# Splitting the attention output product into three fp32r passes, with the second layer's weights loaded late, in a two-layer kernel on one Trainium2 core

## What is computed

```python
def reference(...):
    # layer 0: attention, then a mixture of experts
    q = rmsnorm(x @ Wq); k = rmsnorm(x @ Wk); v = x @ Wv           # 16 heads of 64
    bias = -max(i - j, 0) * softplus(omega) * slope * softplus(k.u)  # per head and key
    attn = softmax(q k^T / 8 + bias, causal)
    y = (attn v).reshape(B, T, H * D) @ Wproj                      # 1024 -> 256
    ...
    # layer 1: a memory read (W_K, W1, W2) and a feed-forward with routed blocks
    ...
```

## Time and profile before

| what | value |
|---|---|
| time, median of 3 runs | 1443.78 us (1443.22 to 1446.7) |
| the profiled execution | 1444.28 us, its span 1442.5 us |
| PE busy | 1380.5 us, 96% of the span, 9680 instructions |
| DVE busy | 991.6 us, 69% |
| ACT busy | 915.8 us, 63% |
| mean granted TensorE clock | 0.98 of full |
| data moved | 122.90 MB, mean 85 GB/s |

### The profile page before, as it was taken

The page is one execution under the profiler, slowest core; times in us unless marked ns, Lnnn a source line. Parts: engine busy times, 40 slices in busy tenths (PEclk is TensorE's granted clock), DMA queues, the critical chain, the costliest instruction groups (busy, mean ns, idle before and its releaser), DMA issues.

```text
span 1442.5 us, 28165 instructions
## 1 busy us (share of the span) xinstructions
PE 1380.5 (96%) x9680; PEld 1087.5 (75%) x9680; DVE 991.6 (69%) x3164; ACT 915.8 (63%) x2292; POOL 168.4 (12%) x562
## 2 busy tenths in 40 slices
PE   4779999999999999999999999999999799999998
PEld 3567778777777777787777777777777578888997
DVE  6938885888588768858875788588578665555442
ACT  5738784878488757848784877578577624433332
POOL 4501110110101101100110111011101100000000
PEclk8879999999999999999999999999999899999999
DMA  6542332232222313222231233132222212111100
GB/s 230 197 146 81 102 97 82 83 113 85 83 81 96 102 63 102 97 76 88 93 104 57 92 113 101 63 100 69 67 94 72 57 57 58 41 41 41 41 16 30
DMA packets 88303, 122.90 MB, mean 85 GB/s; under 512 B 8561, under 2 KB 74466, under 8 KB 88162
## 3 DMA queue, kind: packets, MB, share of 16 engines
q1 hardware_dynamic: 87842, 121.11, 26.1%
q10 hardware_dynamic: 320, 0.00, 0.0%
HBM read 101.69 MB, written 19.40 MB: 84 GB/s over the span
## 4 chain that ended last, share of the span: by engine, by line
PE 87%; ACT 4%; DVE 1%; issue 1%; DMA 0%; SPq 0%; ACTq 0%; DVEq 0%
PE at L799 19%; PE at L808 11%; PE at L884 10%; PE at L859 8%; PE at L925 8%; PE at L1471 7%; PE at L1507 6%; PE at L813 3%; PE at L911 2%; PE at L894 2%; PE at L851 2%; PE at L839 2%; PE at L844 2%; ACT L1065 1%; ACT probT L1056 1%; PE at L1490 1%
## 5 line engine op out<-in xcount | busy, mean ns | idle before, releaser
L1047 ACT ACTIVATE prob<-prob,low 128x512 f32<-128x512 f32 (+3 forms) x512 | 280.6, 550 | 70.9 <-DVE low L1180 70.8
L1180 DVE CUSTOM_DVE_ANT_0 prob<-at,mask 128x512 f32<-128x512 f32 (+3 forms) x512 | 220.5, 487 | 78.9 <-PE at L813 78.9
L1056 ACT ACTIVATE probT<-at 128x512 f32<-128x512 f32 (+1 forms) x256 | 131.6, 541 | 123.2 <-PE at L859 123.1
L808 PE MATMUL at<-kT,qT 64*128 64x512 f32 (+3 forms) x1024 | 194.2, 461 | 8.8 <-DVE up_lo L1233 5.0
L799 PE MATMUL at<-w_hi,cT_lo 128*128 128x386 f32 x512 | 197.5, 386 | 5.1 <-DVE area_raw L1129 4.3
L799 PE MATMUL at<-w_lo,cT_hi 128*128 128x386 f32 x512 | 175.0, 342 | 0.0
L799 PE MATMUL at<-w_hi,cT_hi 128*128 128x386 f32 x512 | 175.0, 342 | 0.0
L859 PEld LDWEIGHTS at<-ident,prob 128*128 128x128 f32 x1280 | 142.4, 141 | 40.0 <-issue 36.7
L859 PE MATMUL at<-ident,prob 128*128 128x128 f32 x1280 | 164.4, 275 | 2.1 <-DVE prob L1193 1.9
L1193 DVE TENSOR_SCALAR prob<-prob,rec 128x512 f32<-128x512 f32 (+3 forms) x512 | 163.3, 383 | 4.5
L884 PE MATMUL at<-probT,v 128*64 128x512 f32 (+3 forms) x1024 | 152.2, 439 | 0.1
(11 more groups left out here) (219 smaller groups left out, 2571.5 us busy)
## 6 DMA issues: line engine op xcount, KB each, us to landing
area_w<-in_L_ffn_w SPq DMA_DIRECT2D x64, 1024.0 KB, 5.5
bias<-in_L_ffn_w SPq DMA_DIRECT2D x160, 32.0 KB, 3.7
x_in<-in_L_attn_x SPq DMA_DIRECT2D x8, 512.0 KB, 6.4
xr<-in_L_attn_x SPq DMA_DIRECT2D x8, 512.0 KB, 4.1
eo_d<-eo SPq DMA_DIRECT2D x32, 128.0 KB, 1.8
x_d<-xr SPq DMA_DIRECT2D x8, 512.0 KB, 2.9
area_raw<-x_d SPq DMA_DIRECT2D x8, 512.0 KB, 4.1
out<-area_raw SPq DMA_DIRECT2D x8, 512.0 KB, 3.0
```

The costliest lines, as they stand in the source:

```text
L808: eng.matmul(bS[i][:, at:at + (c + 1) * P], qT[rows, c * P:(c + 1) * P], kT[rows, 0:(c + 1) * P], start=True, stop=False)
L1047: eng.activation(sl, sl, ACT.Exp, scale=-1.0, bias=low[:, i:i + 1], accum_out=den[:, i:i + 1]).then_inc(exp_done.sem, 1)
L1056: eng.activation(probT[h][:, x:y], bR[i][:, 0:y - x], ACT.Copy).then_inc(done.sem, 1)
L1180: eng.tensor_tensor_reduce(out=prob[s % 2][h][:, off[c]:off[c + 1]], in0=bS[i][:, at:at + (c + 1) * P], in1=mask[:, (NT - 1 - c) * P:T], s ...
```

## The change

The change does these things.

- `output` runs three fp32r matmuls where one fp32 matmul stood: (`yT_lo`, `wp_hi`), (`yT_hi`, `wp_lo`), (`yT_hi`, `wp_hi`), 24 for one n and 96 for a batch.
- `Wproj` goes to `proj_in` in stage 1 and is split there in two halves: two ACT copies of 128x1024 (in the last two rounds, b = 6 and 7) and two POOL subtractions.
- ACT's `copy_y` now writes `yT_hi`, and a new `copy_y` on DVE subtracts it from the bank to get `yT_lo`. `y_done` is now signalled by DVE. The DVE step stands between `divide(s, 0)` or `add_bias` and `copy_q`.
- To make room, the second layer's weights have no tiles of their own. `w1n` is loaded in turn 55 into the token tiles of even batches, `w2n` in turn 62 into `area_w1`, and `rn`, `m1n`, `m2n`, `wk` at the end of turn 63 into `area_w2`, when the last expert is done. `qkn` shares its place with `sq`, for which ACT's `square` gets a wait on `turn_k` of the pair before.
- The jobs have another order: first the four of `w1n`, the four of `w2n`, then the small ones; one job in each slot of turns 62 and 63, and four in turn 64. `scores_210` waits for the job of slot 0 in place of slot 1's. Job 8 waits for the four small loads, and the last job also for the one before it.

```diff
-        w_proj=sb("w_proj", [P, HP, C]),
+        wp_hi=sb("wp_hi", [P, HP, C], F32R),
+        wp_lo=sb("wp_lo", [P, HP, C], F32R),
...
+                    if b >= 6:
+                        half_h = slice((b - 6) * (H // 4), (b - 5) * (H // 4))
+                        eng.wait_ge(wp_load.sem, wp_load.at(0))
+                        eng.activation(wp_hi[:, half_h, :], proj_in[:, half_h, :], ACT.Copy).then_inc(wp_hi_done.sem, 1)
...
+                        eng.tensor_tensor(wp_lo[:, half_h, :], proj_in[:, half_h, :], wp_hi[:, half_h, :].bitcast(F32), ALU.subtract)
...
-        qkn = sb("qkn", [P, NT, 4 * D])
+        qkn = sq
...
-        jobs_at = {(NTURN - 2, 0): (0, 1), (NTURN - 2, 1): (2, 3), (NTURN - 2, 2): (4,), (NTURN - 2, 3): (5,),
-                   (NTURN - 1, 0): (6,), (NTURN - 1, 1): (7,), (NTURN - 1, 2): (8,), (NTURN - 1, 3): (9,),
-                   (NTURN, 0): (10,), (NTURN, 1): (11,)}
+        jobs_at = {(NTURN - 2 + n // 4, n % 4): (n,) for n in range(8)}
+        jobs_at.update({(NTURN, 0): (8, 9), (NTURN, 1): (10, 11)})
...
+                    if s == NTURN - 1:
+                        eng.wait_ge(pe_eo.sem, pe_eo.at(E - 1))
+                        for dst, src in ((rn, t["L1_ffn_router_w"]), (m1n, t["L1_attn_W1"]),
+                                         (m2n[:, :, :], t["L1_attn_W2"].rearrange("(k p) m -> p k m", p=P)),
+                                         (wk[:, :, :], t["L1_attn_W_K"].rearrange("(k p) c -> p k c", p=P))):
+                            eng.dma_start(dst, src).then_inc(small_load.sem, 16)
...
-                    for n in jobs_at.get((s, 1), ()):
+                    for n in jobs_at.get((s, 0), ()):
                         eng.wait_ge(prep_done.sem, prep_done.at(n))
...
-                        m = eng.matmul(bQ[n % 2][:, 0:C], yT[:, h, n * P:(n + 1) * P], w_proj[:, h, :],
-                                       start=(h == 0), stop=(h == HP - 1))
+                        for y, w in ((yT_lo, wp_hi), (yT_hi, wp_lo), (yT_hi, wp_hi)):
+                            m = eng.matmul(bQ[n % 2][:, 0:C], y[:, h, n * P:(n + 1) * P], w[:, h, :],
+                                           start=(h == 0 and y is yT_lo), stop=(h == HP - 1 and y is yT_hi and w is wp_hi))
...
+                        if n == 8:
+                            eng.wait_ge(small_load.sem, small_load.at(0))
+                        if srcs is None:
+                            eng.wait_ge(prep_done.sem, prep_done.at(n - 1))
...
-                    eng.activation(yT[:, s % HP, :], bY[:, :], ACT.Copy).then_inc(y_done.sem, 1)
+                    eng.activation(yT_hi[:, s % HP, :], bY[:, :], ACT.Copy).then_inc(y_hi_done.sem, 1)
...
+                def copy_y(s):
+                    eng.wait_ge(pe_o.sem, pe_o.at(s // HP - 1))
+                    eng.wait_ge(y_hi_done.sem, y_hi_done.at(s))
+                    eng.tensor_tensor(yT_lo[:, s % HP, :], bY[:, :], yT_hi[:, s % HP, :].bitcast(F32), ALU.subtract).then_inc(y_done.sem, 1)
...
                     if begins_in(s) is not None:
                         add_bias(begins_in(s))
+                    if s > 0:
+                        copy_y(s - 1)
                     prepare(s, 2)
```

More of the change, by code:

```diff
@@ L145, in attention_constants @@
         q_scale=sb("q_scale", [P, 1]),
[L146 to L147 removed]
+        **tokens, **early,
         qaug=sb("qaug", [P, T], F32R),
@@ L159, in second_layer_inputs @@
     return dict(
-        w1n=sb("w1n", [P, HC, C]),
-        w2n=sb("w2n", [P, KC, HC * P]),
-        wk=sb("wk", [P, KC, C]),
-        m1n=sb("m1n", [M1, C]),
-        m2n=sb("m2n", [P, KC, M1]),
-        rn=sb("rn", [NB, C]),
         rb=sb("rb", [P, NB]),
@@ L205, in route_tokens @@
         raw_w = sb("raw_w", [P, KC, 3, H * D])
+        proj_in = sb("proj_in", list(wp_hi.shape))
         u_in = sb("u_in", [P, H, D])
@@ L585, in attend @@
     HC, M1, NB = g["HC"], g["M1"], g["NB"]
-    w1n, w2n, wk, m1n, m2n, rn, backT = (g[k] for k in ("w1n", "w2n", "wk", "m1n", "m2n", "rn", "backT"))
+    backT = g["backT"]
     ident = g["ident"]
     xnT_hi_d, xnT_lo_d, x1_d = g["xnT_hi_d"], g["xnT_lo_d"], g["x1_d"]
-    w_hi, w_lo, w_proj, mask, pos, omega, q_scale, W = (g[k] for k in (
-        "w_hi", "w_lo", "w_proj", "mask", "pos", "omega", "q_scale", "W"))
+    w_hi, w_lo, wp_hi, wp_lo, mask, pos, omega, q_scale, W = (g[k] for k in (
+        "w_hi", "w_lo", "wp_hi", "wp_lo", "mask", "pos", "omega", "q_scale", "W"))
     xT_hi, xT_lo, qaug, kaug, ag, tok, bias2 = (g[k] for k in ("c_hi", "c_lo", "qaug", "kaug", "ag", "tok", "bias2"))
@@ L622, in attend @@
         rec = sb("rec", [P, 2 * NT])
-        area_y = sb("area_y", [P, HP * T])
-        yT = area_y[:, :].rearrange("p (h n) -> p h n", h=HP)
+        outs, hidden32 = share(nc, ctx, "area_y", (("yT_hi", [P, HP, T], F32R), ("yT_lo", [P, HP, T], F32R)),
+                               (("hT", [P, HC, T], F32),))
+        yT_hi, yT_lo = outs["yT_hi"], outs["yT_lo"]
         xr = sb("xr", [P, NT, C])
@@ L682, in attend @@
         sp, m1T, rT, number = (l2[k] for k in ("sp", "m1T", "rT", "number"))
-        jobs = [((m1T[:, :, :],), M1, [m1n[:, k * P:(k + 1) * P] for k in range(KC)]),
-                ((rT[:, :, :],), NB, [rn[:, k * P:(k + 1) * P] for k in range(KC)]),
-                ((backT[0:M1, :],), P, [m2n[:, k, :] for k in range(KC)])]
+        w1n = [g["w1n0"], g["w1n1"]]
+        w2n = area_w1[:, :].rearrange("p (k f) -> p k f", k=KC)
+        wk = area_w2[:, 0:KC * C].rearrange("p (k c) -> p k c", k=KC)
+        m2n = area_w2[:, KC * C:KC * C + KC * M1].rearrange("p (k m) -> p k m", k=KC)
+        at = KC * (C + M1)
+        m1n, rn = area_w2[0:M1, at:at + C], area_w2[0:NB, at + C:at + 2 * C]
+        jobs = []
         for k in range(KC):
@@ L689, in attend @@
                 jobs.append(((up_hi[:, k, h:h + 4, :], up_lo[:, k, h:h + 4, :]), P,
-                             [w1n[:, h + i, k * P:(k + 1) * P] for i in range(4)]))
+                             [w1n[h // 4][:, i, k * P:(k + 1) * P] for i in range(4)]))
         for h in range(0, HC, 2):
@@ L693, in attend @@
                          [w2n[:, k, (h + i) * P:(h + i + 1) * P] for i in range(2) for k in range(KC)]))
-        jobs.append(((readT_hi[:, :, 0:M1], readT_lo[:, :, 0:M1]), M1, None))
+        jobs += [((rT[:, :, :],), NB, [rn[:, k * P:(k + 1) * P] for k in range(KC)]),
+                 ((backT[0:M1, :],), P, [m2n[:, k, :] for k in range(KC)]),
+                 ((m1T[:, :, :],), M1, [m1n[:, k * P:(k + 1) * P] for k in range(KC)]),
+                 ((readT_hi[:, :, 0:M1], readT_lo[:, :, 0:M1]), M1, None)]
         wide = [n for n in range(len(jobs)) if len(jobs[n][0]) == 2]
@@ L767, in _ @@
                         second.get_x(eng, 0)
+                    if s == NTURN - HP - 1:
+                        eng.wait_ge(pe_q.sem, pe_q.at(NTURN - HP - 1))
+                        for i in range(2):
+                            eng.dma_start(w1n[i][:, :, :], t["L1_ffn_w1"][i * 4 * P:(i + 1) * 4 * P, :].rearrange(
+                                "(h p) c -> p h c", p=P)).then_inc(w1n_load.sem, 16)
+                    if s == NTURN - 2:
+                        eng.wait_ge(pe_h.sem, pe_h.at(E - 1))
+                        eng.dma_start(w2n[:, :, :], t["L1_ffn_w2"].rearrange("(k p) f -> p k f", p=P)).then_inc(w2n_load.sem, 16)
                     if ends_in(s) is not None:
```

44 lines of the change are left out of this document (23 added, 21 removed).

## The result

The changed kernel took 1456.19 us in the median of 8 runs (1452.78 to 1460.19), the kernel before 1445.24 beside it (1443.1 to 1450.79). The ratio is 1.0067, 95% interval 1.0044 to 1.009; timed again beside another experiment it was 1.0085 (1.0065 to 1.0106). So the change makes the kernel slower by some 11 us, where 7.3 were forecast. The profiled execution took 1458.74 us, 2.5 above the median, with a span of 1457.0.

A forecast was written before the change was run, and what follows sets the result against it. The prediction took TensorE's own list and its waits to bound the kernel (87% of the span). Its terms, 24.3 - 17.5 + 0.5 + 0 = +7.3 us, moved the median from 1443.78 to 1451.1 us, range 1443 to 1459.

The forecast's parts named there:

- The output blocks, -2.5 each: Output blocks: 96 fp32r passes take 11.4 us where 32 fp32 matmuls took 13.91; seven blocks gain 17.5 us.
- The low half of y, +24.3: Turns: turn_aug waits for DVE's subtraction, 0.94 us after ACT's copy; new waits of 0.16 to 0.80 us, 24.3 in all.
- The steps queued behind it: Turns: copy_q and divide(s, 1) stand behind the waiting DVE step; their delay was costed at nothing.
- Rivals 1 to 3: 1: wait covered, 1426.8 us, chance 0.11; 2: clock falls in turns, 1476, 0.04; 3: passes not quicker, 1468.6, 0.03.
- Rival 4: Main case with low bounds, 20 us in the turns and -4 at the end: 1442.8 us, no measurable difference, chance 0.15.
- Stage 1, +0.5, bound 2.1: Stage 1: ACT's first proj_in copy delays the last logits copy by some 0.5 us, between 0 and 2.1.
- POOL is idle: Stage 1: the second half's ACT copy falls into a longer wait for PE, and POOL is idle; no loss added.
- The end of stage 2, 0 from -5.8 + 7.5 - 1.7: End of stage 2: earlier probabilities, late loads and a shorter last product sum to 0, bounds -4 and +4.
- -5.8: End of stage 2, (a): scores_210 waits for an earlier job, so PE and DVE reach the last probabilities 5.8 us earlier.
- +7.5: End of stage 2, (b): job 8 waits 3.9 us for late loads, part at half clock; output(0) starts 7.5 us later.
- -1.7: End of stage 2, (c): the last batch's product is 2.5 us shorter, partly hidden by DVE's normalisation: 1.7 us.
- 30 us in the turns: Turns: upper bound of the low half of y's loss, allowing 0.05 us more in each hand-over.

The follow-up runs named there:

- the profile with the early clock: Changed kernel with both subtractions for the low output weights behind VectorE's last operation of stage 1: 1452.36 us, ratio 1.0056.
- the early loads: Changed kernel with the four small second-layer loads one turn earlier: 1449.58 us, ratio 1.0032; with y also split on GpSimd from SBUF: 1427.82 us, ratio 0.9881.

## Why the prediction was right, and where not

- **The output blocks, -2.5 each: right.** 11.48 us for 13.91 in the timeline, 2.40 by the run with fp32 matmuls, -16.8 for -17.5. The row of another stage with the same shape was the right price.
- **The low half of y, +24.3: right, term by term.** The distances grew by 0.31, 0.31, 0.80 and 0.18 us for 0.32, 0.32, 0.80 and 0.16, and taking the subtraction away gave 24.1 back. DVE's operation has a median of 691 ns over 64, so the row of 687 was right. The 658 ns that the prediction took from the Trainium skill, "VectorE: DVE Perf Modes", section on the TRN2 errata, are 33 short of it; the same section has 691 ns for an fp32 `tensor_tensor` of 512 columns, and that row agrees. The steps queued behind it, `copy_q` and `divide`, did cost nothing, as costed.
- **Rivals 1 to 3** fall by the same rows: nothing covered the wait, the granted clock was 1.00 from 117 to 1115 us, and the passes are quick. Rival 4 falls with the measured size.
- **Stage 1, +0.5, bound 2.1: measured +4.9, mostly not by the change.** In the changed kernel's profile 3.2 us stand in front of the last logits, where the granted clock was lower, and up to 0.6 behind stage 1. What the change costs there is 0.9 us of standstill (2.1 in other runs) and 0.2 of ScalarE's second copy; the first, the part that the 0.5 was costed from, cost nothing in this profile. The step that was wrong is "POOL is idle": it looked at GpSimd's own time and not at what its two subtractions do to DVE beside them. With the standstill the term would have been 1 to 2 us.
- **The end of stage 2, 0 from -5.8 + 7.5 - 1.7: the mechanisms were right, with a scatter of 3 us by the clock.** From `turn_q(61)` to `turn_p0` of turn 64 it went from 55.33 to 51.07 us, -4.3 and not -5.8: the division stood still beside the masks, and the run with the masks moved gives 1.4 of it back. From `turn_p0` to the merge step it went from 6.17 to 15.95, +9.8 and not +7.5: the loads landed later (a wait of 4.63 us for 3.9), and the half clock held from there until the merge step, also over `values`, which I had left out of it. Where the clock came back before the products, it went to 12.97, +6.8. From the first merge step to the second it is 17.41 for 19.76, -2.35 for -1.7. The sum is +3.2 here and +0.2 in the profile with the early clock, both inside the bounds of 4.
- **The sum.** The profiled spans differ by 14.5 us: +7.1 in the turns, +4.9 at the start, +3.2 at the end, -0.6 in the rest. The profiled run of the changed kernel was a long one; between the medians it is 11.0. The turns gave what was forecast, +7.1 for +6.8. The other 4 us fit the standstill (0.9 to 2.1) and the end of stage 2 (0.2, or some 3), an estimate from the profiles, for the medians can't be split. That the range, up to 1459, held the median is partly luck: its upper end came from 30 us in the turns, which they did not cost, and it covered terms that were missing elsewhere.

What stays open: why the granted clock from 40 to 60 us differs between runs from 0.59 to 0.91, whether the change has a part in it, and how often the clock is back early behind the late loads (in two of eight profiles here).

## What to carry to other kernels

Where one copy frees a bank and becomes two steps on two engines, the second step with both hand-overs is paid in every turn: 0.94 us here, of which the slack took 0.14 to 0.78. Copy the bank out whole with one instruction, release it, and split in SBUF on an engine with time to spare; together with the early loads that turned a loss of 11 us into a gain of 16. Before giving an idle GpSimd a wide pass, look at what DVE does beside it, and after every removed wait look at which wide operations now fall together. A load that an end of a stage waits for costs its own wait, and in six of eight profiles 2 to 3.5 us more in TensorE's clock.
